# Attention: the piece of the side bank ahead of the scores for the maxima

## What is computed

```python
def _L0_attn_ref(x, Wq, bq, Wk, bk, Wv, bv, Wo, bo, head_mask):
    q = (x @ Wq.T + bq).reshape(b, s, HEADS, HEAD_DIM)      # 16 heads of 8
    k = (x @ Wk.T + bk).reshape(b, s, HEADS, HEAD_DIM)
    v = (x @ Wv.T + bv).reshape(b, s, HEADS, HEAD_DIM)
    attn = jnp.einsum('bqhd,bkhd->bhqk', q, k) / np.sqrt(HEAD_DIM).astype(np.float32)
    attn = jax.nn.softmax(attn, axis=-1)
    attn = attn * head_mask[None, :, None, None]
    out = jnp.einsum('bhqk,bkhd->bqhd', attn, v).reshape(b, s, HIDDEN)
    return out @ Wo.T + bo

x = x + 0.5 * _L0_ffn_ref(_layernorm(x), ...)
x = x + _L0_attn_ref(_layernorm(x), ...)
x = x + 0.5 * _L0_ffn_ref(_layernorm(x), ...)
```

## Time and profile before

| | us |
|---|---|
| median of 3 runs | 1905.31 (1900.88 to 1912.67) |
| the profiled execution | 1900.91 |
| its span | 1899.1 |

### The profile page before, as it was taken

One profiled execution on the slowest core, in us unless ns is written; L12 is line 12 of the kernel. 1 busy time (PEld: TensorE's weight loads), 2 busy tenths in 40 slices (PEclk: granted clock), 3 DMA queues, 4 the chain that ended last, 5 costly groups with the idle time before them and its releaser, 6 DMA issues. The chain is left out here.

```text
span 1899.1 us, 30193 instructions
## 1 busy us (share of the span) xinstructions
PE 1755.1 (92%) x9569; PEld 1100.5 (58%) x9600; DVE 1391.1 (73%) x2393; ACT 1237.0 (65%) x1914; POOL 891.2 (47%) x878
## 2 busy tenths in 40 slices
PE   5999999999968888888888888888889999999999
PEld 4887878787843333333333333333368787878776
DVE  5666766676758888888888888888457666766674
ACT  4666566656537777777777777776756566656654
POOL 5666666666732222232333322231146566656665
PEclk9999999999969999999999999999899999999999
DMA  3000100010020111111111111110001010000000
GB/s 101 23 22 25 34 22 23 21 33 22 29 81 2 53 53 54 53 54 53 53 54 53 53 42 54 53 48 24 7 28 34 23 34 12 33 22 33 11 22 12
DMA packets 42270, 69.60 MB, mean 37 GB/s; under 512 B 8508, under 2 KB 10036, under 8 KB 42164
## 3 DMA queue, kind: packets, MB, share of 16 engines
q1 hardware_dynamic: 37360, 66.20, 10.5%
q0 software_dynamic: 4096, 1.08, 0.3%
q10 hardware_dynamic: 708, 0.98, 0.1%
HBM read 28.36 MB, written 12.58 MB: 22 GB/s over the span
## 5 line engine op out<-in xcount | busy, mean ns | idle before, releaser
L934 POOL TENSOR_TENSOR ffn_hid_low<-ffn_hidden,ffn_hid_high 128x512 fp32r<-128x512 f32 x448 | 580.1, 1295 | 367.8 <-ACT ffn_hid_high L860 366.5
L1489 DVE TENSOR_REDUCE attn_neg_max<-attn_p_score 128x2 f32<-128x1024 f32 x512 | 623.4, 1223 | 120.1 <-PE attn_p_score L1201 118.0
L1341 ACT ACTIVATE attn_exps<-attn_p_score 128x1024 f32<-128x1024 f32 x512 | 520.4, 1025 | 217.2 <-PE attn_p_score L1187 215.4
L851 ACT ACTIVATE ffn_silu<-ffn_p_gate 128x512 f32<-128x512 f32 x448 | 266.1, 594 | 269.4 <-PE ffn_p_gate L748 267.5
L994 DVE TENSOR_TENSOR ffn_gated<-ffn_silu,ffn_p_up 128x512 f32<-128x512 f32 x352 | 241.3, 686 | 176.3 <-PE ffn_p_up L748 121.2
L860 ACT ACTIVATE ffn_hid_high<-ffn_hidden 128x512 fp32r<-128x512 f32 x448 | 280.8, 627 | 123.4 <-DVE ffn_hidden L1001 121.3
L1201 PE MATMUL attn_p_score<-k_pack,q_pack 32*128 32x512 f32 x1024 | 259.6, 506 | 53.1 <-ACT attn_exps L1341 37.4
L1218 PE MATMUL attn_p_o<-attn_exps,values 128*32 128x512 f32 x2048 | 278.0, 614 | 6.8 <-ACT attn_o_raw L1347 2.5
L1187 PE MATMUL attn_p_score<-q_pack,k_pack 32*128 32x512 f32 x1024 | 254.0, 503 | 1.5 <-DVE attn_neg_max L1489 1.5
L1001 DVE TENSOR_TENSOR ffn_hidden<-ffn_gated,ffn_p_spread 128x512 f32<-128x512 f32 x352 | 241.4, 686 | 17.8 <-remote 5.6
L1187 PEld LDWEIGHTS attn_p_score<-q_pack,k_pack 32*128 32x128 f32 x1024 | 95.1, 184 | 265.6 <-issue 236.9
(11 more groups left out here) (213 smaller groups left out, 2069.0 us busy)
## 6 DMA issues: line engine op xcount, KB each, us to landing
q_pack<-attn_q_high SPq DMA_DIRECT2D x32, 256.0 KB
k_pack<-attn_k_high SPq DMA_DIRECT2D x32, 256.0 KB
feed_x_in<-in_x SPq DMA_DIRECT2D x16, 256.0 KB, 2.8
ffn_x_res<-in_x SPq DMA_DIRECT2D x16, 256.0 KB, 3.4
after_ffn<-ffn_x_out SPq DMA_DIRECT2D x16, 256.0 KB, 2.0
attn_x_in<-after_ffn SPq DMA_DIRECT2D x16, 256.0 KB, 2.8
k_pack<-attn_k_low SPq DMA_DIRECT2D x16, 256.0 KB
q_pack<-attn_q_low SPq DMA_DIRECT2D x16, 256.0 KB
```

Of the source, the lines that this page charges most:

```text
L851: nc.scalar.activation(silu[f % 2][0:n, :], p_gate[f % 2][0:n, :], ACT.Silu).then_inc(silu_ready, 1)
L934: nc.gpsimd.tensor_tensor(hid_low[s][0:n, :], hidden[s][0:n, :], hid_high[s][0:n, :].bitcast(F32), ALU.subtract).then_inc(low_ready, 1)
L1341: nc.scalar.activation(exps[n % len(exps)][:], score_bank("exp", b, n)[:], ACT.Exp, scale=inv_sqrt)\
L1489: V.tensor_reduce(neg_max[g % 2][:, j:j + 2, t], score_bank("max", b, n)[:], AX.X, ALU.max, negate=True).then_inc(max_read, 1)
```

## The change

In half 0 of each unit, the piece is sent behind `score_exp` and ahead of `score_max`, where it was behind both. Half 1 stays: both kinds of scores, then the values product. Nothing else changes in what any engine executes.

```diff
                     for half in range(2):
                         score_exp(b, u, half)
+                        if half == 0:
+                            pieces(b, u, is_first, is_last)
                         if there(ahead):
                             score_max(ahead, v, half)
                         if half == 0:
-                            pieces(b, u, is_first, is_last)
-                        elif u > 0:
+                            continue
+                        if u > 0:
                             times_values(b, u - 1)
                         elif not is_first:
                             times_values(a, UNITS - 1)
```

## The result

The changed kernel took 2033.8 us (median of 4 runs, 2023.8 to 2041.8) against 1905.1 (1900.9 to 1912.7): ratio 1.067, 95% interval 1.061 to 1.073. The profiled execution took 2035.1 us with a span of 2033.3, against 1900.9 and 1899.1.

What follows compares the result with a forecast made beforehand. No engine being full, a loop of waits (E0, ScalarE, M1, V) was taken to bound the attention. 1901 + 81 for waits + 59 for the low clock = 2041, given as 2040 us; range 1950 to 2170.

Steps and rivals of the forecast that it cites:

- The order on the array: In the 14 units with a piece, M0 stands behind it and before E1; this step was taken as 0.21 us.
- M0: Scores for the maxima, half 0 of a unit, on TensorE; the step the change moves behind the piece.
- E1: Scores for the exponentials, half 1 of a unit, on TensorE.
- M1: Scores for the maxima, half 1 of a unit, on TensorE; before the change it starts at +1.61 us.
- V: The product with the values, at a unit's end on TensorE; 1.00 us at full clock, 1.86 at the low one.
- The prediction's upper bound: Step between score groups on the array at most 0.43 us; only units 4 and 12 grow further, 7 us in all.
- E0: Scores for the exponentials, half 0, first in each unit on TensorE; the next unit's was to wait for M0's maxima.
- What is late next: VectorE works in order, so late maxima of M0 delay what later pieces wait for; unit 3 4.61 instead of 3.23 us.
- (c): Rival: the loop over ScalarE covers everything M0 loses and VectorE catches up, 1905 us; chance 0.03.
- (d): Rival: pieces start without M0's wait for ScalarE and units drop to 3.04 us, 1873 us; chance 0.03.
- The clock: In mid-attention, a low stretch of 17 us, costing 4.9 us, in 12 of the 16 batches: 59 us.
- (b, 2340): Rival: the clock falls early in the attention and hardly comes back, batches of 78 us; chance 0.13 (over 2170).

Runs made afterwards that it cites:

- the kernel with the filled waits: The full change plus matmuls of no use between E0 and the piece in units 3, 5, 7, 8 and 11: 1980.2 us, ratio 1.041.

## Why the prediction held

**The batch.** Forecast 50.4 + 5.5 us; measured at the full clock 55.70 (718.08 to 773.78), 5.3 more. By unit, forecast and measured: unit 3 4.61 and 4.68, unit 4 3.40 and 3.34, unit 5 3.86 and 3.83, unit 7 4.36 and 4.42, unit 8 4.15 and 4.04, unit 11 4.25 and 4.29, unit 12 3.36 and 3.30. Units 1, 2, 6, 9, 10, 14, 15 and 0 kept their 3.04 to 3.19; unit 13 took 3.19, forecast 3.21. All waits together were forecast at 81 us, and the kernel with the filled waits puts them at 76. The mechanism was the one forecast, and not only the number.

**The order on the array.** The step from M0 to E1 is 0.34 and not 0.21, but E1, with M1 beside it, is followed by V after 0.33 and not 0.43: 0.66 to 0.67 for what was taken as 0.64. The sizes were off and made up for each other. The prediction's upper bound, by which the array's order (1.86) and the maxima of M0 (1.85) end a unit at the same time, did not come: by the order the next E0 would start 0.66 + 1.00 = 1.66 behind M0. In unit 3 above it starts 1.91 behind it, in units 4 and 5 of the same batch 1.82. So the maxima end these units, by 0.16 to 0.25 us.

**What is late next.** This carried the sum, and the two half changes show it: with M0 moved only in units 2, 6 and 10, unit 3 waits 1.68 us; with it moved only in the units that wait, unit 3 waits its old 0.71 and lasts 3.70. The rivals of no change (c) and of a gain (d) fell with it.

**The clock.** It does fall, and costs 54 us where 59 were forecast. But the shape was another: 12 stretches of 17 us were assumed, 24 came, most of 3 to 10 us and the longest in mid-attention 17; together they are 198 us more than before, near the assumed 204. A microsecond at the low level costs 54 / 198 = 0.27 us, as 4.9 / 17 = 0.29 said. So the price per microsecond was well founded on rows; the number and length of the stretches were a choice, and that their product came out right is luck. Two fifths of the loss hang on it. The reason given for the fall was half right: the long wait does it, also behind E0 and M0 together; that the lone E0 counts was an assumption that nothing here bears out. Where all waits were short (units 1, 9, 13, 14 moved), lone E0s left the clock at 1.00. The waits of 0.92 and 1.00 us in units 7 and 11, which the prediction counted among those that bring it down, had no stretch begin at them.

The rival of a clock that hardly comes back (b, 2340) did not come: over the attention the clock was 0.87. The kernels with the product ahead of E1 came near that time, with a clock of 0.70 in one, but only in part through the clock.

## What to carry to other kernels

Before an instruction is moved ahead of another on one engine, look up who reads the one that becomes late, what stands behind that reader in its engine's own order, and which later instruction waits for that: here 0.97 us of delay in one unit came back as 0.97 in the next, though the unit itself kept its length. Sum these and then look whether they leave TensorE idle for longer than any wait it has now, because the clock can take more: here 54 us on top of 76. The cheap way out was the other list: VectorE does the division that TensorE waits for ahead of maxima whose scores aren't there yet, -0.8%, with TensorE's list as it was.

## What the runs showed of the hardware

Added work made this kernel faster: 6 + 4 + 2 + 3 + 3 matmuls of no use in a batch took 54 us off 2034. The waits ended when they did before, and from 692 to 1249 us every batch was as long (55.7 us) as one at the full clock was without them; what changed is the clock.

A wait of 1.68 us in a batch, with both kinds of scores ahead of it, brought the clock down for 3.4 us (a product of 1.93 us instead of 1.06) in 8 of 13 batches; in the other 5 the same wait passed at the full clock. In the kernel with M0 moved in the waiting units only, waits of 1.32 and 1.14 us, there behind a lone E0, were enough as well.

Shorter waits of the same kind left it alone: 0.70 to 0.73 us in the kernel before, 0.91 and 1.00 behind E0 and M0 together (units 7 and 11 of the kernel with M0 moved ahead of the division), and 0.92 and 1.00 behind a lone E0 in the full change. But in the kernel with the product ahead of E1, which at the full clock waits 0.88 us in most units and up to 1.13 in some, the clock was at its low level for about two thirds of the time from 650 to 1350 us. So the length of one wait doesn't settle it alone, and it was not varied by itself; what else in the stream decides is open.
